# The forward row transform of an attention kernel's image loop: one float32 product becomes two float32r products of split column sums

## The reference, cut to what matters

```python
for _ in range(LEVEL):
    cur, h, v, d = _dwt2(cur)
    details.append((h, v, d))
...
    rec = _idwt2(rec, h * w[:, 0, None, None], v * w[:, 1, None, None], d * w[:, 2, None, None])
...
encR = jnp.einsum('bnd,de->bne', encoding, R)
scores = jnp.einsum('bnd,bmd->bnm', encR, encoding)
A = jax.nn.softmax(scores + mask, axis=2)
return jnp.einsum('bnm,bmd->bnd', A, encoding)
```

## Time and profile before

| | |
|---|---|
| median of three runs | 849.37 us (848.91 to 852.34) |
| the profiled execution | 848.66 us, its span 846.9 us |
| mean granted TensorE clock | 0.935 of full speed |
| PE, DVE, ACT, POOL busy | 731.4, 581.0, 453.7, 464.9 us |
| first forward transform starts, last one starts | 58.9 us, 303.8 us |

### The profile page before, as it was taken

One profiled execution on the slowest core, in us unless ns is written; L12 is line 12 of the kernel. 1 busy time (PEld: TensorE's weight loads), 2 busy tenths in 40 slices (PEclk: granted clock), 3 DMA queues, 4 the chain that ended last, 5 costly groups with the idle time before them and its releaser, 6 DMA issues.

```text
span 846.9 us, 15591 instructions
## 1 busy us (share of the span) xinstructions
PE 731.4 (86%) x4349; PEld 616.0 (73%) x4349; DVE 581.0 (69%) x1951; ACT 453.7 (54%) x998; POOL 464.9 (55%) x744
## 2 busy tenths in 40 slices
PE   6977999999999993332589999999989999999994
PEld 3754676676676662231489899998989989999994
DVE  3844888888888876888878667575675756744431
ACT  1003667777777775200446656666556665566551
POOL 0035767767777755400614846648466484755623
PEclk9987999999999998555699999999999999999998
DMA  9500022122122122800203433435234352333212
GB/s 340 209 3 1 26 76 74 50 74 74 50 74 74 50 75 75 167 26 5 73 33 51 141 45 78 107 50 146 42 84 97 48 147 44 93 90 52 39 21 31
DMA packets 47752, 64.32 MB, mean 76 GB/s; under 512 B 14096, under 2 KB 40784, under 8 KB 47056
## 3 DMA queue, kind: packets, MB, share of 16 engines
q1 hardware_dynamic: 34704, 46.54, 16.7%
q0 software_dynamic: 12800, 17.12, 12.6%
q10 hardware_dynamic: 192, 0.00, 0.0%
HBM read 38.12 MB, written 25.53 MB: 75 GB/s over the span
## 4 chain that ended last, share of the span: by engine, by line
PE 34%; DVE 12%; issue 6%; POOL 3%; ACT 3%; DMA 1%; POOLq 0%; DVEq 0%; ACTq 0%; SPq 0%
PE bank L884 15%; PE bank L898 13%; DVE ge L1243 3%; PE bank L910 2%; PE bank L873 2%; DVE Tc L1259 1%; DVE yl L1359 1%; DVE ohu L1311 1%; POOL out L530 1%; ACT bank L667 1%; DVE jk L1336 1%; POOL yg L508 1%; POOL w2l L494 1%; PE bank L863 1%; DMA raw<-in_fc1T 1%
## 5 line engine op out<-in xcount | busy, mean ns | idle before, releaser
L530 POOL DMA_INDIRECT out<-ob,sidx x72 | 114.0, 1583 | 159.6 <-ACT ob L683 148.0
L1366 DVE TENSOR_TENSOR hl<-bank,hh 128x384 fp32r<-128x384 f32 (+1 forms) x192 | 97.5, 513 | 139.2 <-ACT hh L670 135.5
L667 ACT ACTIVATE bank<-bank,b1s 128x384 f32<-128x384 f32 (+1 forms) x192 | 99.5, 518 | 138.1 <-PE bank L884 131.7
L884 PE MATMUL bank<-yh,w1h 128*128 128x384 f32 (+1 forms) x384 | 132.8, 346 | 8.8 <-DVE hl L1366 5.7
L884 PE MATMUL bank<-yh,w1l 128*128 128x384 f32 (+1 forms) x384 | 123.7, 322 | 0.0
L884 PE MATMUL bank<-yl,w1h 128*128 128x384 f32 (+1 forms) x384 | 123.2, 321 | 0.0
L898 PE MATMUL bank<-w2h,hh 128*128 128x256 f32 x384 | 108.0, 281 | 0.0
L898 PE MATMUL bank<-w2l,hh 128*128 128x256 f32 x384 | 108.0, 281 | 0.0
L508 POOL DMA_INDIRECT yg<-rows,idx x72 | 72.5, 1007 | 64.6 <-issue 59.4
L898 PE MATMUL bank<-w2h,hl 128*128 128x256 f32 x384 | 107.9, 281 | 0.0
L670 ACT ACTIVATE hh<-bank 128x384 fp32r<-128x384 f32 (+1 forms) x192 | 87.8, 457 | 6.1
(11 more groups left out here) (223 smaller groups left out, 1785.9 us busy)
## 6 DMA issues: line engine op xcount, KB each, us to landing
BIG<-in_x SPq DMA_DIRECT2D x4, 2048.0 KB, 19.0
out<-Bs SPq DMA_DIRECT2D x32, 256.0 KB, 2.2
rows<-Yp SPq DMA_DIRECT2D x32, 256.0 KB, 2.4
raw<-in_fc1T SPq DMA_DIRECT2D x16, 512.0 KB
raw<-in_fc2T SPq DMA_DIRECT2D x16, 512.0 KB
yg<-rows,idx POOLq DMA_INDIRECT x72, 2.8
out<-ob,sidx POOLq DMA_INDIRECT x72, 3.8
gwb<-in_gate_w SPq DMA_DIRECT2D x1, 1024.0 KB, 12.4
```

The source lines that it names most:

```text
L530: g.indirect_dma_start(out=out_rows, out_offset=tok(ap=sidx[job.eh][0:m, t:t + 1], axis=0), in_=ob[t % 3][0:m, :], in_offset=None, compute ...
L667: A.activation(h[:, 0:cur.w], h[:, 0:cur.w], ACT.Gelu_apprx_tanh, bias=b1s[:, bass.ds(cur.e, 1), f]).then_inc(s["hact"], 1)
L884: last = T.matmul(Lb[ring(cur, f)][:, 0:cur.w], w1s[cur.eh][i][:, d, f * P:(f + 1) * P], yT[cur.p][k][:, d, 0:cur.w], start=(n == 0), stop ...
L1366: v.tensor_tensor(hT[cur.p][1][:, f, 0:cur.w], Lb[ring(cur, f)][:, 0:cur.w], hT[cur.p][0][:, f, 0:cur.w], ALU.subtract).then_inc(s["hlo"], 1)
```

## The change

The product of L792 is replaced by two products in float32r that add up in the same PSUM bank, of the same rounded `fwdr` with a high part `Xh` and a low part `Xl` of the column sums. ScalarE makes `Xh` by a copy of 128 x 512 (`columns_high`), one step ahead; GpSimd makes `Xl` by a subtraction of 128 x 512 (`rest`), one step ahead, between the statistics and `columns`. The column sums themselves are made two steps ahead in place of one. `Xh` and `Xl` lie where `gwb` lay.

```diff
--- before.py
+++ after.py
@@ -169,7 +169,6 @@
         Pr = [cut(388) for _ in range(2)]
 
         hc = [sb(f"hc{i}", [P, NH, D]) for i in range(4)]
-        gwb = sb("gwb", [P, NE, D])
         clsb = sb("clsb", [P, D])
         ET = [sb(f"ET{i}", [P, 2, NT]) for i in range(2)]
 
@@ -208,6 +207,14 @@
         cbn = sb("cbn", [P, 6])
         cpw = sb("cpw", [P, 4])
         cgl = sb("cgl", [P, NE])
+        fwdr = sb("fwdr", [P, P], F32R)
+
+        opening = ExitStack()
+        gwb = opening.enter_context(nc.sbuf_tensor("gwb", [P, NE, D], F32))
+        opening.close()
+
+        Xh = [sb(f"Xh{i}", [P, NH * D], F32R) for i in range(2)]
+        Xl = [sb(f"Xl{i}", [P, NH * D], F32R) for i in range(2)]
         phase.close()
 
 
@@ -225,7 +232,7 @@
 
         names = """ld_const ld_x0 ld_x1 ld_x2 ld_x3 ld_par ld_band0 ld_band1 ld_band2 ld_band3 ld_bias ld_cls cvt wp wp_part wp_v rep lg_mm lg_m lg_r z_mm z_c z_e bw_t bw_c w8_mm w8
             cls_d cls_p cls_a cls_t et0 et_cls g_cls cls_st cls_g zero
-            xc xc_l z_done zw inv q h0 st0_b st0 var pow nrm st_set hcE et et_ev er er_ev eg_ev sm nmax pexp pt pt_ev av u h1 rv
+            xc xc_l xhi xlo fwdr z_done zw inv q h0 st0_b st0 var pow nrm st_set hcE et et_ev er er_ev eg_ev sm nmax pexp pt pt_ev av u h1 rv
             st1_b st1 tug teg base yp tab base_st0 base_st1 yp_st0 yp_st1
             gt_c gt_t gt_v vt_st vsp_t vsp thr tc cn t_tried t_range t_next tk_c tk_mm oh_begun oh_first
             ohd smm smc ixc ixd wld0 wld1 bld0 bld1 whi wlo0 wlo1 hhi hlo yhi yr gat00 gat01 gat02 gat10 gat11 gat12 yt_t yt hmm hact om oadd omul omt oev obk scat0 scat1 scat2 idc""".split()
@@ -253,15 +260,20 @@
             def __init__(self, i, k):
                 self.n, self.p, self.r = i * UNROLL + k, k % 2, k % 4
                 self.h = i * (UNROLL // 2) + k // 2
+                self.at = i, k
+
+            def plus(self, d):
+
+                return Step(self.at[0], self.at[1] + d)
 
         HEAD, TAIL = 4, 28
 
-        def steps(eng, emit):
+        def steps(eng, emit, ahead=1):
 
 
             def images(i, k, bounded):
                 return [Step(i, k)] + [Step(i, k + d) if not bounded or 0 <= k + d < NB else None
-                                       for d in range(1, -LAG - 1, -1)]
+                                       for d in (ahead, *range(0, -LAG - 1, -1))]
             for k in range(HEAD):
                 emit(*images(0, k, True))
             with eng.Fori(HEAD // UNROLL, TAIL // UNROLL) as i:
@@ -433,7 +445,7 @@
             def columns(m):
 
                 after(po, "xc", m.n)
-                after(po, "z_done", m.n - 1)
+                after(po, "xlo", m.n - 1)
                 xv = XS[:, :, :, bass.ds(m.n, 1), :].rearrange("p h g b c -> p h g (b c)")
                 x0, x1 = xv[:, :, :, 0::2], xv[:, :, :, 1::2]
                 dst = Xc[m.p]
@@ -445,6 +457,13 @@
                 po.wait_ge(s["xc_l"], m.n * 2 + 2)
                 g.tensor_tensor(dst[:, :, 0:32], L2[:, :, 0::2], L2[:, :, 1::2], ALU.add)
                 g.tensor_tensor(dst[:, :, 32:64], L2[:, :, 0::2], L2[:, :, 1::2], ALU.subtract).then_inc(s["xc"], 1)
+
+            def rest(m):
+
+                po.wait_ge(s["xhi"], m.n + 1)
+                after(po, "z_done", m.n - 1)
+                g.tensor_tensor(Xl[m.p][:, :], Xc[m.p].rearrange("p h c -> p (h c)"), Xh[m.p][:, :], ALU.subtract)\
+                    .then_inc(s["xlo"], 1)
 
             def emit(t, nxt, _a, b, _c, d, m):
                 st = ST[t.p]
@@ -478,14 +497,18 @@
                 g.tensor_tensor(N6[t.p][:, 0:4], st[:, 8:12], nm[t.p][:, :], ALU.mult)
                 g.tensor_tensor(N6[t.p][:, 4:6], st[:, 12:14], nm[t.p][:, 2:4], ALU.mult)
                 g.tensor_scalar(O1[t.p][:, :], st[:, 10:12], 1.0, None, ALU.add).then_inc(s["nrm"], 1)
+                if not isinstance(t.n, int) or t.n < NB - 1:
+                    rest(t.plus(1))
                 if nxt:
                     columns(nxt)
                 g.tensor_copy(TST[:, bass.ds(t.n, 1), :].rearrange("p b k -> p (b k)"), st[:, :]).then_inc(s["tab"], 1)
             for q in range(4):
                 po.wait_ge(s[f"ld_x{q}"], 16)
             columns(Step(0, 0))
+            columns(Step(0, 1))
+            rest(Step(0, 0))
             po.wait_ge(s["st_set"], 2)
-            steps(po, emit)
+            steps(po, emit, 2)
 
             def low(eh, q, layer, half):
 
@@ -580,11 +603,22 @@
             act.wait_ge(s["cls_d"], 3)
             A.activation(cgl[:, :], cgl[:, :], ACT.Tanh).then_inc(s["cls_a"], 1)
 
+            def columns_high(m):
+
+                act.wait_ge(s["xc"], m.n + 1)
+                after(act, "z_done", m.n - 1)
+                after(act, "xlo", m.n - 1)
+                A.activation(Xh[m.p][:, :], Xc[m.p].rearrange("p h c -> p (h c)"), ACT.Copy).then_inc(s["xhi"], 1)
+            A.activation(fwdr[:, :], cst("fwd"), ACT.Copy).then_inc(s["fwdr"], 1)
+
+            act.wait_ge(s["cls_d"], 2)
+            columns_high(Step(0, 0))
+
             act.wait_ge(s["z_c"], 3)
             A.activation(z2[:, 1:NJ], z2[:, 1:NJ], ACT.Exp)
             A.activation(z2[:, 0:1], zz[:, 0:1], ACT.Exp, scale=-1.0).then_inc(s["z_e"], 1)
 
-            def emit(t, _nxt, _a, b, c, d, m):
+            def emit(t, nxt, _a, b, c, d, m):
                 if isinstance(t.n, int) and t.n == EARLY + 7:
                     act.wait_ge(s["gt_c"], 6)
                     A.activation(GM[:, 0:EARLY, :, :], GL[:, 0:EARLY, :, :], ACT.Tanh).then_inc(s["gt_t"], 1)
@@ -615,6 +649,8 @@
                     act.wait_ge(s["er"], c.n + 1)
                     A.activation(GT[c.p][:, :, NE + 1:], Rb[:, :].rearrange("p (c t) -> p c t", c=2), ACT.Copy)\
                         .then_inc(s["er_ev"], 1)
+                if nxt:
+                    columns_high(nxt)
                 if b:
 
                     after(act, "av", b.n - 3)
@@ -747,6 +783,7 @@
                                     start=(h == 0 and c == 0), stop=(h == NH - 1 and c == ng - 1))
             last.then_inc(s["lg_mm"], 1)
 
+            pe.wait_ge(s["fwdr"], 1)
             pe.wait_ge(s["cls_t"], 1)
             for c in range(2):
                 last = T.transpose(Tb[:, c * P:(c + 1) * P], CX[:, c * P:(c + 1) * P], ident)
@@ -788,9 +825,9 @@
                 if a:
 
                     after(pe, "zw", a.n * 2)
-                    pe.wait_ge(s["xc"], a.n + 1)
-                    T.matmul(Zb[:, :], cst("fwd"), Xc[a.p].rearrange("p h c -> p (h c)"), start=True, stop=True)\
-                        .then_inc(s["z_done"], 1)
+                    pe.wait_ge(s["xlo"], a.n + 1)
+                    T.matmul(Zb[:, :], fwdr[:, :], Xh[a.p][:, :], start=True, stop=False)
+                    T.matmul(Zb[:, :], fwdr[:, :], Xl[a.p][:, :], start=False, stop=True).then_inc(s["z_done"], 1)
                 if d:
 
                     after(pe, "pt_ev", d.n)
```

## The result

The changed kernel took 854.77 us (median of 7 runs, 852.61 to 856.06) against 849.53 us (7 runs, 847.58 to 852.34). The ratio is 1.0062, with a 95% interval of 1.0047 to 1.0078: slower by about 5.2 us. The forecast was 850.7 us with a range of 845.5 to 857.5. The range held, but the forecast's own range of 848 to 854 just did not. "Same" was to mean within 0.5% and had a chance of 0.62; the measured 0.62% lies above that, in the "slower" that had 0.26. The profiled executions differ by 852.61 - 848.66 = 3.95 us; that of the changed kernel is the fastest of its seven.

The account below looks back on a forecast made before the run. A chain of dependences, a 15.65 us round over two image-loop steps, was taken as the bound. 848.66 - 1.5 (first steps) + 2.8 (VectorE's pair) = 849.96, median 0.7 above: 850.7 us, range 845.5 to 857.5.

Parts of the forecast that it names:

- the forecast's own range: Whole kernel: span of the main forecast of 850.7 us, 848 to 854 us; that case had chance 0.48.
- "Same": Whole kernel: time within 0.5%, 4.25 us, of the kernel before; chance 0.62.
- "slower": Whole kernel: the case of GpSimd becoming late and the upper edge of the main forecast; chance 0.26.
- The pair: VectorE's two L1192 instructions, both inputs in SBUF: held up by GpSimd's reads, 0.2 us a step longer, +2.8 us in all.
- two-step round: Image loop, GpSimd statistics through ScalarE, TensorE, VectorE and back: 15.65 us over two steps; added cost x pays x/2 a step.
- L792 in the loop: TensorE's product in the image loop: not on the round, so its 0.4 us a step saved becomes idle time.
- The first steps: Start of the image loop at 1.2 GHz: the cheaper L792 gains 1.5 us, bounds 0 and 3.
- ScalarE's copy: ScalarE between L616 and L623: about 0.6 us, hidden in the wait there; at most 0.1 us on one step in four.
- GpSimd's subtraction: GpSimd right behind nrm: 1.21 us, fits into its idle time before the statistics and leaves 0.38 in the tight steps.
- The clock: TensorE's granted clock in the loop: stays at 1.00, 2.4 GHz, despite a smaller matmul share.
- The sum: Profiled execution: 848.66 - 1.5 + 2.8 = 849.96 us; median of the runs 0.7 above, so 850.7 us.
- GpSimd being late: Rival at the start of L470: GpSimd's idle room used up, 5.6 us on top of the forecast, 856 us; chance 0.22.

Follow-up runs that it names:

- e1: Changed kernel without GpSimd's subtraction and the low product; ScalarE's copy and the high product stay. Ratio to the kernel before 1.0006, four steps 31.90 us.
- e5: Changed kernel with GpSimd's subtraction replaced by an iota and a memset that only write, low part left out; 852.0 us.
- e7: Kernel before, with two more bn_stats of 256 columns on VectorE right behind the pair at L1192; 870.5 us.
- e2: Changed kernel with the float32 product of the kernel before; high and low part still made but unused; 855.7 us.
- e6: Changed kernel with the split and float32r products for images 0 to 2 only, column sums still two images ahead; ratio to the kernel before 1.0003.
- e11: No split at all, only the column sums two images ahead, against the kernel before; ratio 1.0019.
- e3: Changed kernel with the subtraction moved from behind nrm into the column sums, between their second and third pair; ratio to the kernel before 1.0051.
- e4: Changed kernel with the subtraction ahead of the statistics, column sums three images ahead and ScalarE's copy two; 852.9 us.
- e8: Changed kernel with the subtraction and the low product over the first 256 of 512 columns only; 851.6 us.

## Why the prediction was right, and where its sizes were off

- **The pair** was the right place: the loop lost time because GpSimd's subtraction and the shifted column sums hold up L1192's pair (e1, e5). Forecast 1.62, 1.19, 1.26, 1.21; measured 1.88, 1.36, 1.36, 1.42. The term was mis-sized at +0.2 a step; it measured 1.36 / 4 = +0.34. One instruction of the pair takes 0.48 us alone. The second took 0.83 in every step, so the column sum that slips in between costs 0.35, near the forecast 0.31. The first took 1.13, 0.61, 0.61, 0.67: the subtraction held it until 1.03 to 1.05 us behind `nrm` each time. Forecast was 0.99, although the prediction's own 1.21 - 0.17 is 1.04. What was off most were the pair's starts behind `nrm`, taken from the old timeline: 0.56, 1.12, 0.92, 0.97 became 0.38, 0.92, 0.92, 0.85. Timeline of the changed kernel, one instruction of the pair at a time:

```profile
255.17 1.13 DVE L1229 SCALAR_TENSOR_TENSOR H<-ARENA,ST,hc 128x256 f32<-128x256 f32 x1
256.23 0.83 DVE L1229 SCALAR_TENSOR_TENSOR H<-ARENA,ST,hc 128x256 f32<-128x256 f32 x1
```

- **The round.** I named a two-step round and let every addition pay half. That round was there, but the one-step round had only 0.17 us a step of slack, and it ran through the same pair. The step "a cost of x on this round is paid x/2 a step" failed: beyond the slack it is paid in full (e7). It did no harm to the number, and that was luck: for a growth of 1.36 us in four steps, half is 0.68, and the whole less the slack of 4 x 0.17 is 0.68 too. So the change itself does not tell the two prices apart; e7 does. Measured were 0.77. The order and ScalarE's copy by themselves cost 31.90 - 31.67 = 0.23 (e1), more than the 0.09 that is left, so the parts do not simply add up.
- **L792 in the loop** was worth nothing, as forecast (e2).
- **The first steps** gained 2.3 us in the profile and 1.4 us over the runs (e6 against e11); forecast 1.5, with bounds of 0 and 3 for a clock that rises later or earlier. It did rise earlier, so the product's own share is not known.
- **ScalarE's copy** took 0.62 us (forecast 0.6) and cost at most 0.025 us a step, not nothing. **GpSimd's subtraction** took 1.29 us (forecast 1.21) and fitted, with 0.90 us of idle time left, more than the 0.5 forecast, because the steps grew.
- **The clock** was to stay. It did in the loop; at its end it fell earlier (last section).
- **The sum.** Loop: 28 steps x 0.77 / 4 = +5.4 us, first steps -1.4, together +4.0, against +5.2 (4.0 to 6.6 by the interval) measured. The profiled executions add up otherwise: -2.3 us in the first steps, +5.4 in the loop, +1.7 in its last four steps, and -0.8 behind it. The +1.7 goes with the clock: from the last normalised image to the last output of the loop it is 22.7 to 22.8 us in the three traces in which the granted clock fell 17 us or more behind that image (before, e2, e3), and 23.5 to 25.0 in the changed kernel (24.5), e1, e4 to e6 and e8 to e11, where it first fell 5 to 13 us behind it. How often either happens in a kernel is open, since each was traced once; so 1.2 us of the difference of the medians has no place shown.
- **The range** held in part by luck. Its upper end was there for GpSimd being late, which did not come: GpSimd waited before every statistics step. What filled it was a pair that grew more than forecast. One reading of the prediction is a little off: ScalarE's wait before L616 is 26.7 / 30 = 0.89 us by the earlier trace rows, not 0.92; nothing rests on it.

## What to carry to other kernels

When two rounds of different length run through the same instruction, look for the slack of each before you give a cost a share: the time between the last thing an engine could have waited for and the moment it started is that slack, and it was visible here in the kernel before. A long GpSimd operation that reads SBUF must not be put beside a VectorE operation with two SBUF inputs on the critical round, whatever room GpSimd has; and since the two move against each other, a place chosen by the old timeline need not hold in the new one. A cheaper product on an engine that waits buys nothing. And when two prices give the same number for a change, only another experiment can tell which is right.

## What the runs showed of the hardware

The granted clock at the end of the image loop, window of the changed kernel, columns as in the earlier trace rows:

```profile
328.00:332.00 4.00, 1.10 (x6) 0.58 (x4) 3.83 (x13) 2.29 (x7) 1.87 (x5) 0.78 0.39 131
```

In the kernel before it was 1.00, 2.4 GHz, in this window and fell at 333.4 us; in the changed one it fell at 330.2, its mean is 0.78, and the last image's attention products behind it ran at 1.2 GHz. I had expected no change of the clock here. The cheaper product is not what decides it: with the float32 product in the loop it fell at 330.1 us in e11 and 327.9 in e6, and with the split it fell at 337.9 in e3. What does is not shown.

A GpSimd iota of 1024 elements a partition took 0.99 us and a memset of 512 took 0.52, and neither held up VectorE's pair (e5); a subtraction of 512 elements took 1.29 and did. The subtraction let the waiting pair in about 0.2 us before its own record ended (255.82, which is the first instruction's end less its 0.48 alone, against 256.02).
